# Delta rule in blocks of 16 tokens on TensorE instead of token by token on VectorE, in a one-core transformer kernel

## The reference, cut to what matters

```python
k = k / (norm(k, axis=-1) + 1e-06)          # per head
beta = sigmoid(x @ Wbeta + bbeta)
def _step(Sm, inputs):                      # scan over 512 tokens
    q_t, k_t, v_t, beta_t = inputs
    Sk = einsum('bhde,bhe->bhd', Sm, k_t)
    delta = v_t - Sk
    Sm = Sm + beta_t[..., None] * einsum('bhd,bhe->bhde', delta, k_t)
    return Sm, einsum('bhde,bhe->bhd', Sm, q_t)
return outputs @ Wo + bo
```

## Time and profile before

| | |
|---|---|
| time, median of three runs | 5421.66 us |
| lowest and highest | 5421.22, 5442.21 us |
| span of the profiled execution, first to last instruction | 5326.3 us |
| VectorE, TensorE busy share | 74%, 62% |
| ScalarE, GpSimd busy share | 38%, 31% |
| transfers | 562.83 MB, mean 106 GB/s |

### The profile page before, as it was taken

The page is one execution under the profiler, slowest core; times in us unless marked ns, Lnnn a source line. Parts: engine busy times, 40 slices in busy tenths (PEclk is TensorE's granted clock), DMA queues, the critical chain, the costliest instruction groups (busy, mean ns, idle before and its releaser), DMA issues.

```text
span 5326.3 us, 69075 instructions
## 1 busy us (share of the span) xinstructions
PE 3319.1 (62%) x20044; PEld 2321.1 (44%) x20044; DVE 3960.7 (74%) x9104; ACT 2021.2 (38%) x4827; POOL 1652.0 (31%) x2669
## 2 busy tenths in 40 slices
PE   6313056175561754416365888787688878887785
PEld 3101034064330643315344665565366655665574
DVE  1999988999889998999935665677566656765543
ACT  3101022132221321103123665665466656665453
POOL 1000001601516014240345214422721154326555
PEclk8655567598665986659777999999799989998998
DMA  1300000264212642136454333441223333443566
GB/s 52 130 36 7 3 12 29 81 188 128 85 35 81 183 132 84 40 108 187 124 156 134 106 100 103 139 124 45 89 88 102 100 121 116 138 124 123 185 209 201
DMA packets 409519, 562.83 MB, mean 106 GB/s; under 512 B 55616, under 2 KB 299456, under 8 KB 408512
## 3 DMA queue, kind: packets, MB, share of 16 engines
q1 hardware_dynamic: 360000, 424.14, 26.0%
q0 software_dynamic: 49152, 134.28, 7.6%
HBM read 349.80 MB, written 208.40 MB: 105 GB/s over the span
## 4 chain that ended last, share of the span: by engine, by line
DVE 45%; PE 30%; issue 9%; ACT 6%; POOL 5%; DMA 3%; SPq 0%; DVEq 0%; ACTq 0%; POOLq 0%
DVE rec L1188 5%; DVE rec L1190 5%; DVE skb L1193 5%; DVE rec L1204 4%; DVE rec L1201 4%; PE psum L1107 4%; DVE region L1196 4%; PE psum L954 3%; DVE region L1305 3%; POOL xbuck L1773 3%; PE psum L1124 2%; PE psum L898 2%; PE psum L1007 2%; PE psum L1039 2%; PE psum L976 1%
## 5 line engine op out<-in xcount | busy, mean ns | idle before, releaser
L1782 POOL DMA_INDIRECT yg<-ybuck,words x512 | 540.4, 1055 | 883.6 <-DMA ybuck<-yrow 415.4
L1107 PE MATMUL psum<-xgT,w 128*128 128x128 f32 x4400 | 633.9, 291 | 27.8 <-DMA w<-in_w13T 9.2
L1107 PEld LDWEIGHTS psum<-xgT,w 128*128 128x128 f32 x4400 | 578.0, 204 | 59.5 <-issue 48.1
L1773 POOL DMA_INDIRECT xbuck<-srow,words x512 | 527.9, 1031 | 152.5 <-issue 126.2
L886 PE MATMUL psum<-w_ident,xn 128*128 128x128 f32 x512 | 106.6, 345 | 727.0 <-ACT xn L1495 718.4
L1124 PE MATMUL psum<-w_w2T,hid 128*128 x1100 | 378.2, 427 | 285.0 <-DVE hid L1462 212.9
L1305 DVE TENSOR_REDUCE region<-psum 128x1 f32<-128x384 f32 (+3 forms) x704 | 418.4, 634 | 151.8 <-PE psum L979 149.3
L1664 ACT ACTIVATE xgT<-psum 128x256 f32<-128x256 f32 x662 | 253.3, 383 | 669.0 <-PE psum L1089 667.3
L1754 POOL TENSOR_SCALAR_AFFINE_SELECT region<-region 128x128 f32<-128x128 f32 x1024 | 286.4, 298 | 526.4 <-ACT region L1629 514.8
L1629 ACT ACTIVATE region<-psum 128x512 f32<-128x512 f32 (+3 forms) x1024 | 389.9, 453 | 156.8 <-PE psum L996 151.5
L1134 DVE SCALAR_TENSOR_TENSOR sil<-sil,psum 128x128 f32<-128x128 f32 (+1 forms) x418 | 123.5, 296 | 394.3 <-ACT sil L1679 372.3
(11 more groups left out here) (210 smaller groups left out, 7598.1 us busy)
## 6 DMA issues: line engine op xcount, KB each, us to landing
w<-in_w13T SPq DMA_DIRECT2D x550, 256.0 KB, 3.0
xg<-xbuck SPq DMA_DIRECT2D x662, 128.0 KB, 2.4
ybuck<-yrow SPq DMA_DIRECT2D x662, 128.0 KB
xbuck<-x SPq DMA_DIRECT2D x40, 512.0 KB, 5.3
x_scratch<-res SPq DMA_DIRECT2D x64, 256.0 KB, 2.1
acc<-x_scratch SPq DMA_DIRECT2D x128, 128.0 KB
xbuck<-srow,words POOLq DMA_INDIRECT x512
yg<-ybuck,words POOLq DMA_INDIRECT x512
```

The source lines that it names most:

```text
L1107: o = e.matmul(psum[:, mi, half], w13[I % 3][:, k, half], xgT[I % 2][:, k, :], start=(k == 0), stop=(k == 1), skip_group_check=True)
L1773: e.indirect_dma_start(xbuck[g % 2], bass.IndirectOffsetOnAxis(ap=posu[g % 2][:, J - ROWS0[g], k:k + 1], axis=0), srow[J % 2], None).then_ ...
L1782: e.indirect_dma_start(yg[y % 5], None, ybuck[g % 2][0:TILES_OF[g] * 128, :], bass.IndirectOffsetOnAxis(ap=posu[g % 2][:, j, k:k + 1], axi ...
```

## The change

Rows of `x` are reordered on the way in, so that a tile of 128 rows is 8 batches x 16 tokens: tiles 0 to 31 are batches 0 to 7, tiles 32 to 63 are batches 8 to 15. Inside a tile the recurrence is written as products: the pairs k·k and k·q of the 16 tokens of each (batch, head), the inverse of the 16x16 unit triangle by substitution in 15 rows, and the state carried from tile to tile. Scaling k and v by the square root of beta replaces the factor beta. Products are 32x32 blocks (two batches) on the four diagonal strips of the array. The planner now has three strands for layer A: `project` (rate 1.4), `solve` (1.1) and `chain`, one step a turn; `heads`, `tiles` and `sums` get 1.4, 1.0 and 0.7 a turn. The second attention waits only for the sums of the unit that holds its batch's last tokens (unit 7 for batches 0 to 7). Its input is read with eight transfers per batch.

```diff
-HEAD_RATE, TILE_RATE, SUM_RATE, PROJECT_RATE = 0.6, 0.5, 0.35, 0.15
+HEAD_RATE, TILE_RATE, SUM_RATE, PROJECT_RATE, INVERSE_RATE = 1.4, 1.0, 0.7, 1.4, 1.1
...
+                put("d_send", m)
+            pT.give(xi, "pvm", 2 * n + 2)
+            yield LIGHT
+            put("d_fetch", n)
...
+    def solve():
+        for n in range(NT // 2):
+            while n not in sent:
+                yield LIGHT
+            for _ in range(4):
+                yield LIGHT
+            for i in range(1, 16):
+                put("d_row", n, i)
+                yield LIGHT
+            put("d_back", n)
+            yield LIGHT
+            yield LIGHT
+            for m in (2 * n, 2 * n + 1):
+                put("d_inverse", m)
+                prepared.add(m)
+                yield LIGHT
+            yield LIGHT
+
+    def chain():
+        for m in range(NT):
+            while m not in prepared:
+                yield LIGHT
+            if m % 32 == 0:
+                put("s_zero", m)
+            ai, af = yield from misc.take()
+            put("s_read", m, ai, af)
+            yield LIGHT
+            put("s_rest", m, ai)
+            yield LIGHT
+            ui, uf = yield from misc.take()
+            put("s_solve", m, ui, uf)
+            yield LIGHT
+            put("s_took", m, ui)
+            misc.give(ui, "ue", m + 1)
+            yield LIGHT
+            if m % 32 < 31:
+                put("s_add", m)
+                yield LIGHT
+                put("s_new", m)
+                yield LIGHT
+            put("d_out", m, ai)
+            yield LIGHT
+            u = m // 4
+            while u >= 6 and u - 6 not in scattered:
+                yield LIGHT
+            put("s_rows", m, ai)
+            misc.give(ai, "od", m + 1)
+            chained.add(m)
+            yield LIGHT
+
+    def first_rows(u):
...
-    for q in range(NQ):
-        for i in range(24):
-            mi, mf = bank()
-            put("l_turn", q, i, mi, mf)
-            misc.give(mi, "ldd" if i % 2 else "lda", 12 * q + i // 2 + 1)
-        ahead = Strand(project(q + 1) if q + 1 < NQ else iter(()))
-        for t in range(128):
-            for part in range(3):
-                put("step", q, t, part)
...
+    ahead, inverse, state = Strand(project()), Strand(solve()), Strand(chain())
+    while not state.done:
+        state.step()
+        streams[0].run(HEAD_RATE)
+        streams[1].run(TILE_RATE)
+        streams[2].run(SUM_RATE)
+        ahead.run(PROJECT_RATE)
+        inverse.run(INVERSE_RATE)
+        zeros.run(0.5)
+    while NB - 1 not in added:
...
-            while 48 + b not in added_up or (b >= 6 and b + 6 not in scattered):
+            while 32 * (b // 8) + 31 not in added_up or (b >= 6 and b + 6 not in scattered):
...
+                for h in range(8 * half, 8 * half + 8):
+                    for x in range(4):
+                        p = strips(x)
+                        o = e.matmul(psum[p, mi, h % 8 * 64:h % 8 * 64 + 64], keo[p, h % 2, h // 2 * 32:h // 2 * 32 + 32],
+                                     kqT[m % NR][p, :, h // 2, :], start=True, stop=True, skip_group_check=True)
...
+            elif name == "s_read":
+                m, mi, mf = u
+                pe.wait_ge(s["new"], m + 1)
+                pe.wait_ge(s["kt"], 3 * m + 2)
                 pe.wait_ge(s[mf[0]], mf[1])
...
+                for g in range(8):
+                    for b in range(2):
+                        for x in range(4):
+                            p = strips(x)
+                            c = g * 32 + b * 16
+                            dst = psum[p, mi, :].rearrange("p (k c) -> p k c", k=2)[:, :, c:c + 16]
+                            o = e.matmul(dst, state[p, 8 * b + g, :], kqT[m % NR][p, :, g, 16 * b:16 * b + 16],
+                                         start=(g == 0 and b == 0), stop=True, skip_group_check=True)
+                o.then_inc(s["sq"], 1)
+            elif name == "s_solve":
+                m, mi, mf = u
+                pe.wait_ge(s["rest"], 2 * m + 2)
+                pe.wait_ge(s[f"inv{m % NR}"], 128 * (m // NR) + 128)
+                pe.wait_ge(s[mf[0]], mf[1])
+                for h in range(H):
+                    for x in range(4):
+                        p = strips(x)
+                        o = e.matmul(psum[p, mi, h * 16:h * 16 + 16], inv[m % NR][p, h, :], restT[p, h * 16:h * 16 + 16],
+                                     start=True, stop=True, skip_group_check=True)
+                o.then_inc(s["um"], 1)
+            elif name == "s_add":
+                m, = u
+                pe.wait_ge(s["ue"], m + 1)
+                pe.wait_ge(s["k01"], m + 1)
+                pe.wait_ge(s["new"], m + 1)
+                for g in range(8):
+                    for b in range(2):
+                        for x in range(4):
+                            p = strips(x)
+                            c = (8 * b + g) * 32
+                            both = ueo[m % 2][p, :].rearrange("p (a c) -> p a c", a=2)[:, :, g * 32:g * 32 + 16]
+                            o = e.matmul(psum[p, STATE, c:c + 32], k01[m % NR][p, b, g * 32:g * 32 + 32], both,
+                                         start=False, stop=True, skip_group_check=True)
+                o.then_inc(s["ds"], 1)
...
-                    e.tensor_tensor(tk[:, :, :, :], S[:, :, :, :], ktt, ALU.mult).then_inc(s["scan"], 1)
-                    if t:
-                        e.tensor_tensor(tq[:, :, :, :], S[:, :, :, :], bc(kq[:, :, t - 1, 16:32], 2, 16),
-                                        ALU.mult).then_inc(s["scan"], 1)
-                    dv.wait_ge(s["scan"], c + 1)
-                    e.tensor_reduce(skb[:, :, :], tk[:, :, :, :], AX.X, ALU.add).then_inc(s["scan"], 1)
-                    if t:
-                        dv.wait_ge(s["scan"], c + 2)
-                        e.tensor_reduce(vo[:, :, t - 1, :], tq[:, :, :, :], AX.X, ALU.add).then_inc(s["scan"], 1)
...
+            elif name == "d_row":
+                n, i = u
+                c = 30 * n + 2 * i - 2
+                t, tmp = tri[n % 2], within(prod[:, 0:2 * i * i], [2, i, i])
+                dv.wait_ge(s[f"fetch{n % 2}"], 256 * (n // 2) + 256)
+                dv.wait_ge(s["clean"], 4)
+                dv.wait_ge(s["inv"], c)
+                e.tensor_tensor(tmp, bc(gram[n % 2][:, :, i, 0:i], 2, i), t[:, :, 0:i, 0:i], ALU.mult).then_inc(s["inv"], 1)
+                dv.wait_ge(s["inv"], c + 1)
+                dv.wait_ge(s[f"back{n % 2}"], 16 * (n // 2))
...
+            elif name == "s_rest":
+                m, mi = u
+                dv.wait_ge(s["sq"], m + 1)
+                dv.wait_ge(s["kt"], 3 * m + 3)
+                e.tensor_tensor(rest, vT[m % NR], psum[:, mi, 0:256], ALU.subtract).then_inc(s["rest"], 1)
+                dv.wait_ge(s["rest"], 2 * m + 1)
+                dv.wait_ge(s["um"], m)
+                e.transpose(restT, rest).then_inc(s["rest"], 1)
+            elif name == "s_new":
+                m, = u
+                dv.wait_ge(s["ds"], updates(m) + 1)
+                dv.wait_ge(s["sq"], m + 1)
...
+                e.tensor_tensor(flat, flat, half32, ALU.pow).then_inc(s["pw"], 1)
...
+            elif name == "d_send":
+                m, = u
+                sp.wait_ge(s["ge"], 2 * m + 2)
+                e.dma_start(pairs_dram[m].rearrange("p (h t) -> p h t", h=H), mine[m % 2]).then_inc(s[f"sent{m % 2}"], 16)
+            elif name == "d_fetch":
+                n, = u
+                for i in range(2):
+                    sp.wait_ge(s[f"sent{i}"], 16 * n + 16)
+                sp.wait_ge(s["inv"], 30 * max(n - 1, 0))
+                for c in range(2):
+                    for b in range(8):
+                        src = pairs_dram[2 * n + c, 16 * b:16 * b + 16, :].rearrange("j (h t) -> h j t", h=H)
+                        e.dma_start(gram[n % 2][16 * b:16 * b + 16, c], src[:, :, b % 2 * 16:b % 2 * 16 + 16]).then_inc(
+                            s[f"fetch{n % 2}"], 16)
...
```

More of the change, by code:

```diff
@@ L174, in normed @@
         return xi, t_xt
-    pblk, pT = Slots([0]), Slots([0])
-    def project(q):
-        for g in range(2):
-            def chunk(n):
-                bi, bf = yield from pblk.take()
-                nth[f"px{bi}"] += 16
-                ready = (f"px{bi}", nth[f"px{bi}"])
-                put("p_in", n, bi, bf)
-                yield LIGHT
-                xi, xt = yield from normed(("block", bi), ready, 2, pT)
-                pblk.give(bi, "xt", xt)
-                for j in range(2):
-                    m = 2 * n + j
+    pblk, pT = Slots([0, 1]), Slots([0, 1])
@@ new lines, in stages, with project @@
+    added, chained, prepared, sent = {}, set(), set(), set()
+    def project():
+        for n in range(NT // 2):
+            bi, bf = yield from pblk.take()
+            nth[f"px{bi}"] += 16
+            ready = (f"px{bi}", nth[f"px{bi}"])
+            put("p_in", n, bi, bf)
+            yield LIGHT
```

(68 more changed lines are left out.)

488 lines of the change are left out of this document (235 added, 253 removed).

## The result

The changed kernel takes 6224.04 us (median of 4 runs, 6215.53 to 6228.82) where the kernel before takes 5425.18 (median of 4): ratio 1.147, 95% interval 1.144 to 1.149. It is slower, where 5000 us (4620 to 5450) was forecast.

What follows compares the result with a forecast made beforehand. VectorE bounds the scan; without it TensorE would bound: 3319 - 69 - 137 + 819 = 3932 us, less 233 gives 3699, at 0.816 4533, plus 327 and 45 is 4905; 95 more gives 5000 us, range 4620 to 5450.

Steps and rivals of the forecast that it cites:

- VectorE added 655 us, some 900 in the phase: New VectorE work, 10.2 us per tile over 64 tiles; some 900 us take the place of 2370 and bound nothing.
- A pair 20 ns: Weight load plus matmul in the new small TensorE products: 40,960 pairs at 20 ns, 819 us.
- the rival of 25 ns: Small TensorE pairs issued no faster than 25 ns apart: 1024 us for them, total 5250; chance 0.18.
- Clock 0.91 when TensorE is fuller: First phase: a fuller TensorE is granted clock 0.91, so its other work shrinks from 1137 to 1000 us.
- the clock's rival: First phase: TensorE's clock stays at 0.69, 396 us more work, 485 after 0.816, total 5485; chance 0.05.
- The share 0.816: TensorE's busy share in the second attention, applied to all work before the last stretch: 3699 us make 4533.
- The rival of in-order queues: Block hand-overs stand behind unrelated work; TensorE's first-phase share 0.70, 370 us more, total 5370; chance 0.10.
- The power 2.8 us: GpSimd's power of 32 elements per tile: about 2.8 us, with the rest some 6 us per tile, 385 us.
- SP at nothing: SP's waits for landings in the solve's DRAM transfers, twice per pair of tiles, about 2 us each, costed at nothing.
- From the chain's end to the span's end 2630 us: Time after the chain's end at 2275 us, up to the forecast span of 4905 us.
- Span to median +95: Whole kernel: the span before, 5326, stands 95 us below the runs' median, 5422; the forecast keeps that difference.
- The side of slower: Strips of different rows don't run side by side; a pair costs up to 65 ns, 7250 us at worst; chance 0.08.

Runs made afterwards that it cites:

- a0_again: The changed kernel itself, unchanged, measured once more beside another run of the kernel before: 5968.61 us, ratio 1.117.
- h1: The changed kernel with the solve train's products issued twice, 8192 more pairs: 6397.63 us, ratio 1.179.
- k1: The changed kernel with preparation spread over more turns, inputs asked for earlier, slower router stream and higher rates beside the second attention: 5179.94 us, ratio 0.971.
- e2: The changed kernel with GpSimd's power replaced by a multiplication of the same shape, leaving out the square roots: 5981.57 us, ratio 1.096.
- k3: k1 with GpSimd's power replaced by a multiplication of the same shape, leaving out the square roots: 4997.10 us, ratio 0.936.
- e3: The changed kernel with each block's input asked for one block earlier, ahead of SP's 16 fetches: 6018.1 us in the profiled execution, no ratio given.
- i1: A version with preparation spread and inputs asked for earlier, its second attention again waiting for all sums of MoE 1: 5544.90 us, ratio 1.040.
- second group: The later runs, on chips or at hours where the kernel before took 5336 to 5341 us.
- first group: The earlier runs, including the changed kernel's first, on chips or at hours where the kernel before took 5422 to 5458 us.

## Why the prediction was wrong, by its own steps

- **VectorE added 655 us, some 900 in the phase**: 955 us. The transposes, for which the trace of before had no row, took 0.40 to 0.45 us (0.42 taken), the solve 10.0 us for a pair of tiles (9.7). Right.
- **A pair 20 ns**: 18 ns by busy time (15.8 in a0_again), 21 to 23 in place by h1. Right on the mean, and the rival of 25 ns is out as a floor. That the row of eight gave 20 was partly luck: eight pairs have seven spacings, so its 0.16 us make 23 ns, as the sum for L1063 had it with fifteen. The trains differ: 128 pairs of 32 columns in 1.29 us (L956) with the clock at 1.00 all that time:

```profile
1199.98 1.29 PE L956 MATMUL psum<-region 32*32 32x32 f32 x128
```

```profile
1199.00:1202.00 3.00, 3.00 (x136) 2.15 (x134) 0.16 (x1) 0.66 (x3) 1.27 (x2) 1.00 0.04 8
```

  Less the passage of one, about 0.2 us as in an L956 matmul's mean of 202 ns, that is 8.5 ns a pair. The 64-column train of L942 above took 3.46 us, near 25 ns, at a granted clock of 0.58.
- **Clock 0.91 when TensorE is fuller**: it was 0.69 as before (0.76 in k1). TensorE's other work is 1981 - 738 = 1243 us, not 1000. The clock explains 137 of that, the shrinking that didn't come. The other 106 are work that took longer or came earlier than in the kernel before: the tiles' first product took 324 us for the same 1896 instructions that had taken 269, and 252 of layer A's 256 output products lie ahead of the phase's end instead of 192. With pairs 81 us cheaper the phase's work is 162 above 1819, or 198 us after 0.816. The first half of the clock's rival, at 5%, came true, the dearer pairs of its second half didn't (its sum is 391 us, not 396).
- **The share 0.816**: the step that failed. It was read from a phase with other work and carried to one whose stages are fewer, longer and dependent. At 0.816 the 1981 us of work would have ended at 45 + 2428 = 2473 us; they ended at 3497, 1024 us of the 1222 by which the phase was missed. In its place TensorE stood at a share of 0.57, and waits for the preparation, 821 us of them, are the largest part of the gap. The rival of in-order queues named the mechanism and gave it 0.70 and a tenth; for its place it looked at the chain, not at the preparation, which the planner lists in a burst. Even k1 reaches only 0.68, near the 0.63 of the thin stretch which that rival had pointed to.
- **The power 2.8 us**: 5.46 us (from 1.13 us for 4 elements to 5.46 for 32, 0.155 us an element). "GpSimd has time enough" was true (929 of 3347 us) and no argument: the power's latency was worth 242 us (e2) and 183 (k3).
- **SP at nothing**: 206 us (e3), because about 4 us of waiting for `d_send` and 7.68 us of issuing stand ahead of an input. I had counted what waits on SP for landings, not SP's own time of 0.48 us for each transfer, and `p_in` not at all among what is behind.
- **Small packets don't bound**: right. 652,848 packets took 26.5% of 16 engines' span, and the share in the phase is 0.29.
- **Second attention 30 to 40 us after the chain**: 30. Right, and i1 shows its worth, 172 us.
- **From the chain's end to the span's end 2630 us** (4905 - 2275): 2726, 96 more, with a tail of 451 us instead of 327 and a little less ahead of it. Right to 4%.
- **Span to median +95**: that was not the kernel's. The span of before, 5326.3 us, is that of an execution of the second group (5327.49 us beside k1), its median one of the first; an execution's time and its span differ by 1 to 2 us in the runs here. 1222 us (chain) + 96 - 95 + 1 make the error of 1224.

The side of slower came true, but not by its mechanism: strips of different rows do overlap.

## What to carry to other kernels

The share of an engine in one phase says what another phase can reach only if the stages of work hang together as loosely there; where one tile's stages cross engines, lay their latencies end to end (here 19 to 24 us) and compare them with the work which the issue order puts between two of them, not with the engines' totals. A transfer's issue time, or a slow operation on an engine with time to spare, is free only if nothing in the same in-order queue, or in the chain behind it, is needed sooner. A change that takes a bound engine away needs its order planned anew: by the order alone nearly the same instructions took from 12% more (a0_again) to 3% less (k1) than the kernel before beside them.

## What was not expected of the hardware

- 32x32 f32 pairs on four strips, with rows and columns of their own, pass every 8.5 ns at a granted clock of 1.00 (128 in 1.29 us). The Trainium skill ("TensorE: Matmul & The Clock Gate", section "Wait — 56ns, not 53.3ns?") says that matmuls start at least about 25 ns apart; this train of 32 columns on four strips disagrees, and the measurement decides for it. As an average in place, h1's 21 to 23 ns, the same number would have done.
- Trains of small products lose TensorE time that no semaphore explains: 249 to 304 us on some chips or at some hours and 84 to 138 on others, for nearly the same instructions. The instruction queue (q8) carried 487 transfers, 7.98 MB, where before it was 171, 2.80 MB, and in a0_again 58 of the 75 pauses over 0.6 us end 2.2 to 2.8 us after one of them starts.
- In the first group, small products pause while GpSimd issues indirect transfers: 242 of the 289 short pauses of the kernel after, but 3 of 15 in a0_again.
- A float power on GpSimd costs 0.155 us for each further element of a partition, 5.46 us at 128x32.
- SP needs 0.48 us to issue a transfer of 64-byte runs, 16 in 7.68 us (median 0.45 for one).
- TensorE at a busy share of 0.58 was granted 0.69 on the mean, and in one train of small pairs 0.58 while it was busy 3.69 of 4 us, where the phase after it, at 0.80, had 0.91.
